# First attention of a two-layer transformer kernel: turn of the layer norm in the scores' banks and later, third context later, fourth query rounding ahead of slot 5

## What is computed

```python
x = x + L0_xattn(layernorm(x), ctx, ctx, mask, wq, wk, wv, wo)   # 32 heads, 8 key/value heads of 128, rope
x = x + L0_ffn(layernorm(x), 4-bit weights, zeros, scales)       # silu(gate) * up, 1376 wide
x = x + L1_xattn(layernorm(x), ctx, mask, ...)                   # rms norm of q and k, no rope
x = x + L1_ffn(layernorm(x), ...)                                # router, top 8 of 128 slots, gate
```

## Time and profile before

| | us |
|---|---|
| median of 3 runs (lowest, highest) | 2425.37 (2425.29, 2427.68) |
| profiled execution, its time | 2425.11 |
| its span, first to last instruction | 2423.3 |
| TensorE busy | 2367.6 (98%) |
| VectorE, ScalarE, GpSimd busy | 1625.1, 1254.1, 1227.8 (67%, 52%, 51%) |
| mean granted TensorE clock | 0.994 of full |

### The profile page before, as it was taken

The page is one execution under the profiler, slowest core; times in us unless marked ns, Lnnn a source line. Parts: engine busy times, 40 slices in busy tenths (PEclk is TensorE's granted clock), DMA queues, the critical chain, the costliest instruction groups (busy, mean ns, idle before and its releaser), DMA issues.

```text
span 2423.3 us, 45113 instructions
## 1 busy us (share of the span) xinstructions
PE 2367.6 (98%) x17668; PEld 1295.6 (53%) x17668; DVE 1625.1 (67%) x3133; ACT 1254.1 (52%) x2423; POOL 1227.8 (51%) x983
## 2 busy tenths in 40 slices
PE   8899999999999999999999999999999999999998
PEld 4455555555555555444444655555555555555554
DVE  7977777777777798754444666667666666656566
ACT  7666555656555545433232554555555555544443
POOL 4656566666666666233232445445555555445531
PEclk9999999999999999999999999999999999999999
DMA  6111121212121111011101011122121212221101
GB/s 211 45 45 36 44 53 27 53 27 53 32 53 31 42 40 28 27 44 36 44 11 29 27 31 28 44 53 62 36 62 36 62 36 62 53 43 27 27 14 70
DMA packets 216753, 108.13 MB, mean 45 GB/s; under 512 B 169280, under 2 KB 192480, under 8 KB 216544
## 3 DMA queue, kind: packets, MB, share of 16 engines
q1 hardware_dynamic: 216544, 105.25, 17.5%
HBM read 61.62 MB, written 4.19 MB: 27 GB/s over the span
## 4 chain that ended last, share of the span: by engine, by line
PE 65%; POOL 13%; DVE 11%; issue 5%; ACT 5%; DMA 0%; POOLq 0%; DVEq 0%; SPq 0%; ACTq 0%
PE PB L865 18%; PE PB L817 16%; PE PB L977 9%; PE PB L801 6%; PE PB L994 5%; POOL AR L2711 5%; POOL AR L2716 3%; POOL PSP L2729 2%; PE PB L907 2%; PE PB L842 2%; DVE AR L2128 2%; DVE WB L1933 2%; PE PB L773 2%; POOL AR L2706 1%; ACT JUNK L1330 1%
## 5 line engine op out<-in xcount | busy, mean ns | idle before, releaser
L865 PE MATMUL PB<-WB,AR 128*128 128x512 f16 x3072 | 685.5, 380 | 3.4 <-DVE XTB L1952 1.6
L817 PE MATMUL PB<-XTB,WB 128*128 128x512 f16 x3072 | 679.5, 380 | 1.2 <-DVE XTB L1952 0.7
L865 PEld LDWEIGHTS PB<-WB,AR 128*128 128x128 f16 x3072 | 298.3, 98 | 359.0 <-issue 11.1
L817 PEld LDWEIGHTS PB<-XTB,WB 128*128 128x128 f16 x3072 | 297.5, 98 | 345.3 <-issue 5.6
L2722 POOL TENSOR_TENSOR AR<-AR,SML 128x512 f32<-128x512 f32 x128 | 144.6, 1150 | 318.1 <-DVE SML L2113 318.1
L2143 DVE SCALAR_TENSOR_TENSOR X<-PB,SML,X 128x512 f32<-128x512 f32 x256 | 189.5, 747 | 169.4 <-PE PB L865 163.4
L1490 ACT ACTIVATE AR<-PB 128x512 f16<-128x512 f32 x256 | 132.0, 602 | 248.2 <-PE PB L907 248.2
L2023 DVE TENSOR_TENSOR AR<-PB,AR 128x512 f16<-128x512 f32 x128 | 88.2, 690 | 167.9 <-ACT AR L1453 167.9
L2711 POOL TENSOR_TENSOR AR<-AR,CST 128x512 f32<-128x512 f32 x128 | 183.0, 1430 | 33.9 <-ACT AR L1400 33.9
L977 PE MATMUL PB<-XTB,AR 128*128 128x512 f16 (+1 forms) x864 | 192.5, 379 | 0.0
L1994 DVE TENSOR_TENSOR AR<-AR 128x512 f16<-128x512 f32 x128 | 132.9, 1038 | 74.7 <-ACT AR L1406 74.5
(11 more groups left out here) (273 smaller groups left out, 3776.9 us busy)
## 6 DMA issues: line engine op xcount, KB each, us to landing
STG<-in_wo SPq DMA_DIRECT2D x14, 1024.0 KB
STG<-in_wq SPq DMA_DIRECT2D x13, 1024.0 KB
STG<-in_qw_gu SPq DMA_DIRECT2D x40, 128.0 KB
STG<-in_ctxT SPq DMA_DIRECT2D x4, 1024.0 KB
X<-in_x SPq DMA_DIRECT2D x4, 1024.0 KB, 10.3
out_x<-X SPq DMA_DIRECT2D x16, 256.0 KB, 2.4
STG<-in_wk SPq DMA_DIRECT2D x14, 256.0 KB
STG<-in_wv SPq DMA_DIRECT2D x14, 256.0 KB
```

Source lines behind the costliest of these rows:

```text
L817: m = pe.do.matmul(b[:, :], wq[x][:, k, h * 128:(h + 1) * 128], XT[y][c][:, k, :], start=n == 0, stop=n == 11)
L865: m = pe.do.matmul(b[:, :], AT[x][:, h, t * 128:(t + 1) * 128], wo[y][:, h, :], start=n == 0, stop=n == 11)
```

## The change

It has four parts, all in the first attention.

- `plan_ln` for L = 0: the norms of the halves go from slots 0 and 3 to 0 and 4, their turns from 2 and 5 to 3 and 6, the lower parts from 2 and 6 to 3 and 6.
- The third context: peak from slot 0 of unit 2 in bank 6 to slot 2 in bank 4, scale from slot 1 to 5, the first lower half from slot 7 to 8. The second stays in 9.
- `ln_banks`: the turned tiles of (0, 2), (0, 3) and (1, 0) use banks 4 and 5 for both halves; before it was banks 2 and 3 for the first half and 1 and 6 for the second.
- ScalarE runs `queries_0(u + 1, 3)` before slot 5 in all units of the first attention, as opposed to after it.

```diff
-            for half, (norm, turn, low) in enumerate(((0, 2, 2), (3, 5, 6))):
+            for half, (norm, turn, low) in enumerate(((0, 3, 3), (4, 6, 6)) if L == 0 else ((0, 2, 2), (3, 5, 6))):
                 plan(L, u, norm, "ln_norm", i, c, half)
                 plan(L, u, turn, "ln_turn", i, c, half)
                 plan(L, u, low, "ln_low", i, c, half)
...
-        plan_at(0, ("c", 2), (1, 9), (2, 0, 6), (2, 1), (2, 7), (2, 9))
+        plan_at(0, ("c", 2), (1, 9), (2, 2, 4), (2, 5), (2, 8), (2, 9))
...
-        IN_FFN = {(1, 2), (1, 3), (2, 0), (2, 1)}
-
         def ln_banks(i, c, half):
             if (i, c) == (1, 1):
                 return 6, 7
...
             if (i, c) == (0, 1):
                 return 2, 3
-            return (4, 5) if (i, c) in IN_FFN else ((2, 3), (1, 6))[half]
+            return ((2, 3), (1, 6))[half] if i == 2 and c > 1 else (4, 5)
...
                     if L == 0:
-                        side(0, u, 5)
                         queries_0(u + 1, 3)
                     elif not k_by_dma(1, u + 1):
                         keys_1(u + 1)
-                    for slot in range(5 if L else 6, 10):
+                    for slot in range(5, 10):
                         side(L, u, slot)
```

## The result

The changed kernel takes 2432.41 us (median of 10 runs, 2426.21 to 2434.35) against 2426.08 for the kernel before (10 runs, 2422.81 to 2427.76). The ratio is 1.0026, with a 95% interval of 1.0017 to 1.0035: slower by a little over what a measurement can tell from no change. The forecast was 2432.1. One of the ten took 2426.21 at a mean granted clock of 0.993, the other nine 2431.35 or more at 0.990 to 0.991; there is no profile of it, so why it was quicker stays open. Two executions of kernels timed later, of 3066 and 9125 us at granted clocks of 0.75 and 0.49, go into no ratio here. The profiled execution has a span of 2431.0 (before 2423.3) at a mean granted clock of 0.991 (before 0.994).

The account below looks back on a forecast made before the run. TensorE, busy 98% of the span, was taken as the bound. The terms -2.3 + 2.7 + 1.4 + 0.4 + 2.4 + 1.6 + 0.8 = +7.0 on 2425.1 gave 2432.1 us, range 2424.0 to 2437.0.

Parts of the forecast that it names:

- Unit 7, -2.3: Keys behind unit 7 start at 292.12 instead of 294.39, with ScalarE's fourth rounding ahead of slot 5: -2.3 us.
- the cover was priced at 0: Other units: weights' roundings end some 2 us later at price 0; without cover at most 0.23 each, 3 in all.
- Unit 2, +2.7: Keys of unit 4 start at 145.7 instead of 143.02, behind the chain at the end of unit 2: +2.7 us.
- The wait before the first turned tile: Unit 2: TensorE waits a new 4.0 us until VectorE has reduced the peak in the shared bank 4.
- its 1.7 falls into the 2.1 of waiting there: 0: Unit 2: the clock loss of 1.7 us behind the 4.0 wait is hidden by 2.1 before the weighing, costing 0.
- a wait of some 2: Sign of being right: before the weighing of units 2 and 4, some 2 us of waiting released by an X addition.
- Unit 4, +1.4 and +0.8: Weighing of unit 4 starts at 202.86 instead of 201.47, +1.4 us; clock loss 0 to 1.7, middle taken, +0.8.
- Unit 28, +0.4: The gate's scale table behind the fourth rounding delays X additions and the weighing of unit 28: +0.4 us.
- Unit 30, +2.4 and +1.6: Unit 30: waits of 1.6 and 3.4, next output product at 977.3 against 974.91, +2.4 us; lower clock, +1.6.
- rival 2: GpSimd gets quicker, its 14.0 us in the first attention nearing 12.5: a wash, 2426 or 2427.6 us; chance 0.18.
- Rival 3: Fourth sum early enough: 4.4 us goes in unit 2, 0.8 in unit 4, 2.3 in unit 8, total 2417.6; chance 0.14.
- Rival 4: More clock: new waits near 2 us also drop the clock, three more times 1.7, 2437 us; chance 0.08.

Follow-up runs that it names:

- the order in unit 7 alone: The kernel before, with ScalarE's fourth query rounding ahead of slot 5 in unit 7 only: 2421.28 us against 2425.79, ratio 0.9984.
- the filled waits: The changed kernel with products nobody reads, nine ahead of unit 4's weighing and fourteen ahead of slot 7 in unit 30: 2428.86 us.
- the peak in bank 2: The changed kernel with the third context's peak product in bank 2 instead of bank 4: 2433.14 us.
- the turn ahead: The changed kernel with ScalarE's slots 5 and 6 ahead of the fourth query rounding in units 2, 4, 30: 2423.26 us; ratio to the kernel before 0.9991.
- the last kernel: The changed kernel with slots 5 and 6 (units 2, 4, 30) and slot 5 (unit 28) before the fourth rounding, peak in bank 2: 2419.05 us, ratio 0.9972.
- the order alone: The kernel before, with only ScalarE's fourth query rounding moved ahead of slot 5 in all units of the first attention: 2427.75 us.

## Why the prediction held, point by point

**Unit 7, -2.3.** Right. The order in all units gives 2.27 here, the order in unit 7 alone 2.27. Nothing was lost where the cover was priced at 0: the shift goes from 3.46 at 297.85 to 3.51 ahead of unit 28.

**Unit 2, +2.7.** The sum was right, the way there only in part, and there is some luck in it. The wait before the first turned tile was put at 4.0 and is 3.70. GpSimd's fourth sum came at 135.6, not 136.1, and VectorE's subtractions ended half a microsecond sooner. But the 2.1 before the weighing, into which the clock's 1.7 was to fall, is not there. The step that failed is "its 1.7 falls into the 2.1 of waiting there: 0". The clock took 3.1 here (1.97 and 4.88 for 1.04 and 2.75), so that the first output product started at 130.91, not 128.1, and TensorE's own pace filled what should have been waiting: VectorE waited 0.55 for it at 142.34. The loss of 3.1 is the odd one; behind the same 3.70 it is 1.5 to 1.8 in three other profiles. In the one of these that keeps the change's order in unit 2 (the filled waits), the clock's loss does fall into the wait, as forecast, and 0.69 is left. The sign "a wait of some 2" before this weighing did not reckon with that: 2.1 less 1.7 leaves 0.4. The keys start at 145.9 either way, because the two chains end within some 0.5 of each other.

**Unit 4, +1.4 and +0.8.** The chain was right (1.26). The clock was between two bounds, none and 1.7, and the middle was taken; it was the upper one, 1.57, and the filled wait gives 1.5. A forecast by ends, each with a chance, would have said more than the middle.

**Unit 28, +0.4.** Right; the wait of 0.33 before the weighing is the X addition.

**Unit 30, +2.4 and +1.6.** Right within 0.3: the waits are 1.56 (1.6) and 3.37 (3.4). The clock's part, 1.6 in the filled run, is the forecast's, though behind nearly the same wait (3.38) output product 3 took 5.30 with the peak in bank 2.

**The rivals.** GpSimd got quicker where rival 2 looked for it, but by less: from head 0 to the fourth sum 13.3 in unit 2, 13.8 in unit 4 (14.0 before). Unit 4 of after, then unit 2 of the kernel before:

```profile
199.37 1.71 POOL L2708 TENSOR_TENSOR AR<-AR,CST 128x512 f32<-128x512 f32 x1
...
198.99 0.96 DVE L1991 TENSOR_TENSOR AR<-AR 128x512 f16<-128x512 f32 x1 [0.80 <-ACT AR L1404]
...
127.28 1.26 POOL L2716 TENSOR_TENSOR AR<-AR 128x512 f32<-128x512 f32 x1
...
127.53 1.29 DVE L1952 TENSOR_TENSOR XTB<-PB,XTB 128x512 f16<-128x512 f32 x2 [0.96 <-ACT XTB L1511]
```

The sine product beside a lower query rounding (SBUF from SBUF) takes 1.71 for 1.27. The sum that has the norm's subtraction (one input in PSUM) beside it for 1.0 us takes 1.26, no longer than the shortest sine product (1.26). By the Trainium skill, "GPSIMD Engine Reference", section Specifications, GpSimd shares its SBUF interfaces with VectorE and contends with instructions that have two SBUF inputs; the trace agrees. Rival 3 needed the fourth sum by 197.5 in unit 4, and it came at 202.4, behind a pass already 2.9 late. Its price also took all 4.4 of waiting in unit 2 away, although the new wait for the peak's bank does not hang on the fourth sum: with the turn ahead alone, where nobody waits behind that sum, the first attention ends 1.3 ahead of before, not 7.5. What rival 3 wanted takes the other order and the other bank: the last kernel, 4.3 ahead there. Rival 4 would have put three more drops of the clock; there was the one in unit 4.

**What was not foreseen at all**: -0.5 behind 1000 us. A wait at the start of the second attention is 1.35 shorter (2.68 at 1443.26, before 4.03 at 1435.06), but it is 3.60 and 2.72 in the two profiles of the turn ahead, and the two profiles of the kernel before differ by 1.3 behind 1000 us. So -0.5 is within chance.

## What to carry to other kernels

A stage that is moved "half a unit later" lands at a place in each engine's queue, not at a time: ask what the instruction just ahead of it waits for, because here two copies, 1.06 us together, stood behind a sum of another engine, and that cost some 9 us in three units, the clock that was lost behind the waits counted in. A wait that is only moved up or down its chain gives nothing back: taking the 3.70 out of unit 2 alone gained nothing, and the wait of 4.98 at the unit's end cost 1.3 more, since the slow weighing behind it had no slack to fall into. Price a wait of TensorE with the clock that it may lose, and give that price a range.

## What the runs showed of the hardware that was not expected

- A wait of 2.42 (205.60, after) was followed by the lower level of the granted clock, 1.2 GHz (0.50 from 205.6 to 208.3); the waits of 1.62 in unit 2 and 1.07 in unit 30 of the kernel before were followed by full speed. The length alone does not tell: behind 2.06 in unit 30 of the order alone the clock stayed at 1.00 (972.4 to 976), and behind 1.55 near 1400 us, with one of 0.37 shortly ahead of it, it fell (0.50 from 1403 to 1406, before).
- The same wait does not cost the same each time. Behind 3.70 in unit 2 the transposes and the query product took 1.97 and 4.88 in after, 1.09 and 4.44 with the turn ahead: 3.1 or 1.7 us over full speed. A second profile of the turn ahead has 1.97 and 3.36, 1.5 over, so it varies between executions of one kernel too.
- Nine products that nobody reads, 2.11 us of them in a wait of 2.4, kept the clock at its upper level (1.00 from 206 to 210) and saved 1.5 us.
